# Coupling's twisted partners by transfers that swap partition halves, and two PSUM banks per instruction

## The chip, the cores and the metric

The kernel runs on one core of one Trainium2 chip. The metric is the time of the whole kernel on the device in microseconds (us). Before the change the median of three runs is 1016.11 us (1016.07 to 1016.4).

## What is computed

A chain of two blocks over x of shape (32, 128, 128): causal attention and a gated recurrence with a coupling network (block 0), then experts, a second attention, an adaptive layer and slot attention (block 1). All is float32. The change lies in the coupling of block 0. Its input x is the hidden state of the recurrence:

```python
def _coupling_net(h, w1, b1, w2, b2, w3, b3, w4, b4):
    h = _gelu(h @ w1 + b1)          # 128 -> 128
    h = _gelu(h @ w2 + b2)          # -> 64
    h = _gelu(h @ w3 + b3)          # -> 32
    return jax.nn.sigmoid(h @ w4 + b4)
def _twist(x):
    o_r, o_i, p_r, p_i = jnp.split(x, 4, axis=-1)
    return jnp.concatenate([p_r, -p_i, -o_r, o_i], axis=-1)
gf = _global_net(x.mean(axis=1, keepdims=True), ...)
out = x
for _ in range(3):
    tf = _coupling_net(out, ...)
    coupling = 0.1 + adaptive_range * (0.7 * gf + 0.3 * tf - 0.5) * 2.0
    out = out + coupling * _twist(out)
```

The coupling coefficient is one number per token in tf and one per sequence in gf; the weights are laid out so that all 128 partitions carry it.

## The kernel before, in words

Features lie on the 128 partitions, the 4096 tokens on the free axis, in eight chunks c of 512. Each engine has its own list of instructions, written out by hand; semaphores order them across engines, and also within an engine where one instruction needs another's result. HF is the hidden state (one 512-column piece a chunk), XT holds the twisted state, XF the running sum of the block, PB the eight PSUM banks of 512 columns.

The coupling takes the chunks in four pairs p = 0 to 3 (chunks 2p and 2p+1) and goes through three cycles y = 0 to 2, twelve couplings m = 4y + p. A coupling has five stages, st 0 to 4, and the pairs follow one another one stage apart (`turn_steps`).

- `pe_h1`, `act_g1` (st 0): first layer, one matmul and one Gelu for each chunk of the pair. The matmul of m >= 4 waits for the sum of m - 4 (`s_cs`), the Gelu of m >= 4 for GpSimd's update of m - 4 (`s_ptw`), since it overwrites H1, which that update reads.
- st 1, 2: second and third layer, both chunks in one bank (L941, L946, L973, L976).
- st 3: fourth layer (L951), a bank for each chunk, and Tanh in place (L981), the sigmoid up to scale and shift.
- st 4, VectorE (`dve_couple`), each step once for each chunk of the pair: first the coefficient cp = Tanh x ar03 + cB in PSUM (L994); for y < 2 second cp x state into H1 (L998); third cp x twisted state in PSUM (L1007); fourth the sum with the state into HF (L1012), in the last cycle with XF (L1015).
- st 4, GpSimd (`pool_couple`): twisted state minus H1 (L1026), and in cycle 1 the state added to XF (L1030).

The twisted state of cycle 0 is made by `pe_tw` (L930, a product with a signed permutation) and `act_tw` (L961, a copy from PSUM to XT). Later cycles update it: twist(out + cp x twist(out)) = twist(out) - cp x out.

Beside this run: the recurrence's gates for chunk 7 on VectorE (L494 to L547), which end just ahead of coupling; the global net (`pe_context`, `act_context`, `dve_context`, L600), the first steps of the adaptive layer (`dve_adapt`, L1065 to L1072), and ten weight splits for the experts, ScalarE's part L1087 and GpSimd's part L1092, one a turn. Behind it the experts begin (`pe_up`, L1169, L1174, L1183), while the last coupling, m = 11, is still done on VectorE between their steps. Which PSUM bank a matmul writes is planned by `plan3`: two rings of four banks, one for the small layers, one for the fourth layer and part of the twist.

## Time and profile before

| | us |
|---|---|
| median of three runs | 1016.11 |
| span of the profiled execution | 1016.5 |
| TensorE, VectorE, ScalarE, GpSimd busy | 977.0, 876.8, 831.3, 471.2 |
| block 0 attention and gates | 0 to 455 |
| coupling | 455 to 525 |
| experts | 525 to 707 |
| second attention and on | 707 to 1016.5 |

The profile is one execution. A line of a timeline gives the start and the length in us, the engine, the line of the kernel, the operation with what it writes and reads, and how many instructions were merged; in brackets stands idle time ahead of it and what ended it. Merged instructions can overlap, so the distance between starts tells how fast an engine goes. The experts' up and down matmuls overlap coupling's end from 509 us. Idle time of an engine off the path costs nothing.

### The profile page before, as it was taken

What the parts mean: (1) busy time and instruction counts of PE and PEld (TensorE: products, weight loads), DVE (VectorE), ACT (ScalarE), POOL (GpSimd) and SP (SyncE); (2) the same over time, 40 slices, a digit from 0 to 9 for tenths busy, and PEclk for the clock granted to TensorE, in tenths of its full rate; (3) what the DMA queues carried; (4) which work ended last, traced back from release to release, by engine and by line L of the source; (5) the groups of instructions that cost most, each with busy time, mean ns of one, the idle gap of its engine ahead of it and who ended that gap; (6) DMA issues with size and microseconds to landing.
All of it is one profiled execution on the core that took longest, in us unless ns stands there. A gap on an engine that the chain in (4) does not pass through costs nothing.

```text
span 1016.5 us, 25956 instructions
## 1 busy us (share of the span) xinstructions
PE 977.0 (96%) x8939; PEld 789.2 (78%) x8939; DVE 876.8 (86%) x3718; ACT 831.3 (82%) x2232; POOL 471.2 (46%) x541
## 2 busy tenths in 40 slices
PE   7999999999999999999989999999999999999897
PEld 6898888888888989743268988888777777776566
DVE  6777989898989888799998899889988888896985
ACT  6888888888888888887797878776887888886786
POOL 2334545454545463606810112102887888893041
PEclk9999999999999999999999999999999999999999
DMA  9000000000000000000000000000000000000002
GB/s 376 35 2 2 2 2 2 2 2 2 2 2 2 2 2 2 2 1 0 1 1 1 1 1 1 1 11 11 23 23 23 23 23 23 23 3 1 1 2 84
DMA packets 8723, 18.31 MB, mean 18 GB/s; under 512 B 1296, under 2 KB 5648, under 8 KB 8208
## 3 DMA queue, kind: packets, MB, share of 16 engines
q1 hardware_dynamic: 8592, 16.65, 4.9%
q8 instruction: 71, 1.16, 0.5%
q14 instruction: 60, 0.49, 0.2%
HBM read 10.36 MB, written 2.10 MB: 12 GB/s over the span
## 4 chain that ended last, share of the span: by engine, by line
PE 79%; DVE 9%; ACT 6%; POOL 3%; issue 3%; DMA 0%; DVEq 0%; ACTq 0%; POOLq 0%
PE PB L245 8%; PE PB L246 8%; PE PB L247 8%; PE PB L341 6%; PE PB L396 6%; PE PB L379 6%; PE PB L1798 5%; PE PB L1195 3%; PE PB L1770 3%; PE PB L1197 3%; PE PB L1196 3%; PE PB L1815 3%; PE PB L428 2%; PE PB L429 1%; PE PB L430 1%
## 5 line engine op out<-in xcount | busy, mean ns | idle before, releaser
L371 POOL TENSOR_TENSOR W<-W,small 128x512 f32<-128x512 f32 x128 | 138.5, 1082 | 216.3 <-DVE small L365 216.3
L360 ACT ACTIVATE W<-W,small 128x128 f32<-128x128 f32 x512 | 198.8, 390 | 29.6 <-DVE small L351 29.0
L245 PE MATMUL PB<-RR_s 128*128 128x256 f32 (+3 forms) x568 | 184.4, 325 | 3.5 <-issue 1.9
L246 PE MATMUL PB<-RR_s 128*128 128x256 f32 (+3 forms) x568 | 176.8, 311 | 0.0
L247 PE MATMUL PB<-RR_s 128*128 128x256 f32 (+3 forms) x568 | 176.7, 311 | 0.0
L351 DVE CUSTOM_DVE_ANT_0 W<-PB,W 128x128 f32<-128x128 f32 x512 | 117.3, 284 | 39.1 <-PE PB L341 38.1
L1786 POOL TENSOR_TENSOR AR_s<-AR_s,small 128x512 f32<-128x512 f32 x128 | 129.3, 1040 | 15.9 <-DVE small L1779 15.8
L1169 ACT ACTIVATE AR_s<-PB,W 128x512 f32<-128x512 f32 (+2 forms) x160 | 100.5, 629 | 28.5 <-PE PB L247 22.1
L245 PEld LDWEIGHTS PB<-RR_s 128*128 128x128 f32 x568 | 108.6, 191 | 11.1 <-issue 4.2
L1183 DVE TENSOR_TENSOR RR_s<-AR_s,RR_s 128x512 fp32r<-128x512 f32 (+2 forms) x160 | 100.4, 636 | 17.1 <-ACT RR_s L1174 13.8
L1779 DVE CUSTOM_DVE_ANT_0 AR_s<-PB,W 128x128 f32<-128x128 f32 x512 | 111.0, 286 | 2.6 <-PE PB L1770 0.9
L246 PEld LDWEIGHTS PB<-RR_s 128*128 128x128 f32 x568 | 108.8, 191 | 4.4 <-issue 0.5
L247 PEld LDWEIGHTS PB<-RR_s 128*128 128x128 f32 x568 | 108.4, 191 | 4.9
L360 ACT ACTIVATION_READ_ACCUMULATOR W<-W,small 128x1 f32 x512 | 96.5, 188 | 0.0
L1804 ACT ACTIVATE AR_s<-PB 128x512 f32<-128x512 f32 x128 | 72.6, 592 | 19.4 <-PE PB L1798 19.0
L1791 ACT ACTIVATE AR_s<-AR_s 128x512 f32<-128x512 f32 x128 | 79.7, 625 | 9.6 <-POOL AR_s L1786 9.2
L310 DVE COPY AR_s<-PB 128x512 f32<-128x512 f32 x128 | 86.0, 672 | 1.2 <-PE PB L247 1.2
L379 PE MATMUL PB<-W 128*128 128x128 f32 x512 | 81.4, 281 | 2.6 <-ACT XT L385 2.4
L1798 PEld LDWEIGHTS PB<-W,AR_s 128*128 128x128 f32 x512 | 57.3, 142 | 26.3 <-issue 12.4
L1798 PE MATMUL PB<-W,AR_s 128*128 128x128 f32 x512 | 71.5, 280 | 5.0 <-ACT AR_s L1822 2.5
L385 ACT ACTIVATE XT<-PB 128x512 f32<-128x512 f32 x128 | 74.1, 579 | 1.2 <-PE PB L379 1.2
L341 PE MATMUL PB<-AR_s 64*128 64x128 f32 x1024 | 74.4, 285 | 0.0
(385 smaller groups left out, 2437.0 us busy)
## 6 DMA issues: line engine op xcount, KB each, us to landing
W<-in_w SPq DMA_DIRECT2D x1, 5809.5 KB, 25.5
W<-in_w SPq DMA_DIRECT2D x2, 1024.0 KB, 7.2
out<-XT SPq DMA_DIRECT2D x8, 256.0 KB, 2.3
XF<-in_xT SPq DMA_DIRECT2D x3, 512.0 KB, 10.9
W<-AR_s SPq DMA_DIRECT2D x16, 64.0 KB, 2.1
AR_s<-AR_s SPq DMA_DIRECT2D x16, 64.0 KB, 2.1
QS<-AR_s SPq DMA_DIRECT2D x12, 64.0 KB, 2.1
KR<-AR_s SPq DMA_DIRECT2D x12, 64.0 KB, 2.1
```

The source lines that it names most:

```text
L245: nc.tensor.matmul(out, lh, rh, start=True, stop=False)
L246: nc.tensor.matmul(out, ll, rh, start=False, stop=False)
L247: return nc.tensor.matmul(out, lh, rl, start=False, stop=True)
L341: mm = nc.tensor.matmul(score(u, h), qk[r, b * 128:b * 128 + 128], qk[r, 256 + b * 128:256 + b * 128 + 128], start=True, stop=True)
L351: nc.vector.tensor_tensor_reduce(SS[r][:, hl], score(u, h), w("mask"), 1.0, 3.0e38, ALU.add, ALU.min, mx[r][:, h:h + 1]).then_inc(s_max, 1)
L360: e = nc.scalar.activation(SS[r][:, hl], SS[r][:, hl], ACTF.Exp, bias=mx[r][:, h:h + 1], scale=-1.0, accum_out=rc[r][:, h:h + 1])
L371: nc.gpsimd.tensor_tensor(s3, s3, over(rc[r], 2, [128, 4, 128]), ALU.mult).then_inc(s_nrm, 1)
L379: mm = nc.tensor.transpose(PB[4][:, hl], SS[u % 6][:, hl], ident)
L1169: nc.scalar.activation(G4[k][:, 0:L], PB[k][:, 0:L], ACTF.Gelu_apprx_tanh, bias=b1).then_inc(s_ge, 1)
L1779: nc.vector.tensor_tensor_reduce(SS5[r][:, hl], score5(u, h), w("mask"), isq8, -3.0e38, ALU.subtract, ALU.max, mx5[r][:, h:h + 1]).then_in ...
L1786: nc.gpsimd.tensor_tensor(s3, s3, over(mx5[r], 2, [128, 4, 128]), ALU.subtract).then_inc(s_sub, 1)
L1798: mm = nc.tensor.transpose(bank5(("p", u))[:, hl], SS5[u % 6][:, hl], ident)
```

## The change

The twist matmuls and copies are gone. The partner of cycle 0 comes by transfers, two for each chunk, that write the upper 64 partitions of HF into the lower 64 of XT and the other way round; SyncE issues them once attention is done with XT, and those of pairs 2 and 3 wait for those of pair 0 and 1. The signs of the twist go to the coefficient: a column `tsign` (1, -1, -1, 1 for the four groups of 32 partitions) multiplies ar07, ar03 and the constant 0.1. The update of later cycles stays as it is, because swapping the halves turns the sign of the coefficient. The PSUM banks are now one tensor, and Tanh as well as each of VectorE's steps takes the pair's two banks in one instruction of 1024 columns, with one count of the semaphore for a pair. GpSimd's instructions stay at 512 columns but wait for the pair. The column `twist` of 128 weights becomes `tsign` of 1. The rest of the diff is the counts of the waits, `pe_tw`, `act_tw`, `plan_tw` and their calls taken out, and the plan of banks without them.

```diff
-        PB = [ctx.enter_context(nc.psum_tensor(f"PB{i}", [128, 512], F32)) for i in range(8)]
+        PS = ctx.enter_context(nc.psum_tensor("PB", [128, 4096], F32))
+        PB = [PS[:, i * 512:(i + 1) * 512] for i in range(8)]
...
-            nc.vector.tensor_scalar(cB[:, a:b], gfT[:, a:b], ar07, 0.1, ALU.mult, ALU.add).then_inc(s_cxd, 1)
+            nc.vector.tensor_scalar(cB[:, a:b], gfT[:, a:b], ar07, c01, ALU.mult, ALU.add).then_inc(s_cxd, 1)
...
-                    nc.vector.tensor_scalar(ar07, w("ar"), 0.7, None, ALU.mult).then_inc(s_set, 1)
+                    nc.vector.tensor_scalar(ar07, w("ar"), w("tsign"), 0.7, ALU.mult, ALU.mult).then_inc(s_set, 1)
+                    nc.vector.tensor_scalar(c01, w("tsign"), 0.1, None, ALU.mult).then_inc(s_set, 1)
...
+        def banks3(key):
+
+            n = through3[key + (0,)][1] % 4
+            assert through3[key + (0,)][0] == 1 and through3[key + (1,)][1] % 4 == n + 1
+            return PS[:, (4 + n) * 512:(6 + n) * 512]
...
             if m < 4:
                 pe.wait_ge(s_gd, c * NGD + GFIN)
             else:
-                pe.wait_ge(s_cs, 2 * (m - 4) + s + 1)
+                pe.wait_ge(s_cs, m - 4 + 1)
...
-        def pe_tw(p):
-            for s in range(2):
-                pe.wait_ge(s_gd, (2 * p + s) * NGD + GFIN)
-                pe_drained3(("tw", p, s))
-                nc.tensor.matmul(bank3(("tw", p, s))[:, :], w("twist"), cs(HF, 2 * p + s), start=True, stop=True).then_inc(s_tw, 1)
...
-        def act_tw(p):
-            for s in range(2):
-                act.wait_ge(s_tw, 2 * p + s + 1)
-                nc.scalar.activation(cs(XT, 2 * p + s), bank3(("tw", p, s))[:, :], ACTF.Copy).then_inc(s_twc, 1)
...
-                for s in range(2):
-                    act.wait_ge(s_h4, 2 * m + 2)
-                    nc.scalar.activation(bank3(("h4", m, s))[:, :], bank3(("h4", m, s))[:, :], ACTF.Tanh, bias=b4h2, scale=0.5).then_inc(s_tn, 1)
+                act.wait_ge(s_h4, 2 * m + 2)
+                nc.scalar.activation(banks3(("h4", m)), banks3(("h4", m)), ACTF.Tanh, bias=b4h2, scale=0.5).then_inc(s_tn, 1)
...
+            cp = banks3(("h4", m))
+            if 0 in steps:
+                dve.wait_ge(s_tn, m + 1)
+                nc.vector.scalar_tensor_tensor(v8(cp), v8(cp), ar03, over(cB[:, 8 * p:8 * p + 8], 2, [128, 8, 128]), ALU.mult, ALU.add).then_inc(s_cp, 1)
             if y < 2 and 1 in steps:
-                for s, cp in enumerate(cps):
-                    dve.wait_ge(s_cp, 2 * m + s + 1)
-                    nc.vector.tensor_tensor(cs(H1[p], s), cp, cs(S, s), ALU.mult).then_inc(s_ct, 1)
...
+                dve.wait_ge(s_cp, m + 1)
+                nc.vector.tensor_tensor(H1[p], cp, S, ALU.mult).then_inc(s_ct, 1)
+            if 2 in steps:
+                dve.wait_ge(s_cp, m + 1)
                 if y == 0:
-                    dve.wait_ge(s_twc, 2 * p + s + 1)
+                    dve.wait_ge(s_tw[p % 2], 64 * (p // 2) + 64)
                 else:
-                    dve.wait_ge(s_ptw, 2 * m + s - 8 + 1)
+                    dve.wait_ge(s_ptw, 2 * (m - 4) + 2)
                 if y < 2:
-                    dve.wait_ge(s_ct, 2 * m + s + 1)
-                nc.vector.tensor_tensor(cp, cp, cs(Tw, s), ALU.mult).then_inc(s_cu, 1)
...
+                    dve.wait_ge(s_ct, m + 1)
+                nc.vector.tensor_tensor(cp, cp, Tw, ALU.mult).then_inc(s_cu, 1)
+            if 3 in steps:
+                dve.wait_ge(s_cu, m + 1)
                 if y < 2:
-                    nc.vector.tensor_tensor(cs(S, s), cp, cs(S, s), ALU.add).then_inc(s_cs, 1)
+                    nc.vector.tensor_tensor(S, cp, S, ALU.add).then_inc(s_cs, 1)
...
             for s in range(2):
-                i = 2 * m + s
-                pool.wait_ge(s_ct, i + 1)
-                pool.wait_ge(s_cu, i + 1)
+                pool.wait_ge(s_ct, m + 1)
+                pool.wait_ge(s_cu, m + 1)
                 nc.gpsimd.tensor_tensor(cs(Tw, s), cs(Tw, s), cs(H1[p], s), ALU.subtract).then_inc(s_ptw, 1)
...
         def sp_layers():
+            sp.wait_ge(s_pv, NV)
+            for p in range(4):
+                if p >= 2:
+                    sp.wait_ge(s_tw[p % 2], 64)
+                for c in (2 * p, 2 * p + 1):
+                    sp.wait_ge(s_gd, c * NGD + GFIN)
+                    nc.sync.dma_start(cs(XT, c)[0:64, :], cs(HF, c)[64:128, :]).then_inc(s_tw[p % 2], 16)
+                    nc.sync.dma_start(cs(XT, c)[64:128, :], cs(HF, c)[0:64, :]).then_inc(s_tw[p % 2], 16)
```

## Rows read from the trace of the kernel before

**Rows 1.** The page's first line.
```profile
span 1016.5 us, 25956 instructions
```

**Rows 2.** Busy time of each engine in a stretch, then granted clock, DMA share, GB/s.
```profile
455.00:481.00 26.00, 24.85 (x74) 8.32 (x75) 25.90 (x46) 20.49 (x38) 16.81 (x16) 1.00 0.00 0
...
525.00:707.00 182.00, 181.83 (x913) 159.14 (x914) 163.12 (x317) 144.73 (x251) 22.32 (x22) 1.00 0.01 4
```

**Rows 3.** Timeline of VectorE, coupling m = 0 and the steps behind it.
```profile
455.36 1.40 DVE L994 SCALAR_TENSOR_TENSOR PB<-PB,small 128x512 f32<-128x512 f32 x2
456.67 1.28 DVE L998 TENSOR_TENSOR AR_s<-PB,HF 128x512 f32<-128x512 f32 x2
457.86 1.28 DVE L1007 TENSOR_TENSOR PB<-PB,XT 128x512 f32<-128x512 f32 x2
459.06 1.28 DVE L1012 TENSOR_TENSOR HF<-PB,HF 128x512 f32<-128x512 f32 x2
460.25 1.01 DVE L1065 TENSOR_SCALAR small<-W,small 32x128 f32<-32x128 f32 x1
461.29 0.28 DVE L1067 TENSOR_TENSOR small<-small,W 32x128 f32<-32x128 f32 x1
...
461.82 1.40 DVE L994 SCALAR_TENSOR_TENSOR PB<-PB,small 128x512 f32<-128x512 f32 x2
...
466.82 0.85 DVE L600 TENSOR_SCALAR small<-small 128x8 f32<-128x8 f32 x1
```

**Rows 4.** Timeline of GpSimd: the updates of m = 0, 4 and 7.
```profile
458.69 2.49 POOL L1026 TENSOR_TENSOR XT<-XT,AR_s 128x512 f32<-128x512 f32 x2 [1.15 <-DVE PB L1007]
...
481.31 2.49 POOL L1026 TENSOR_TENSOR XT<-XT,AR_s 128x512 f32<-128x512 f32 x2
...
499.17 2.51 POOL L1026 TENSOR_TENSOR XT<-XT,AR_s 128x512 f32<-128x512 f32 x2
```

**Rows 5.** Timeline of ScalarE: first layer of m = 11, Tanh of m = 11.
```profile
501.76 1.26 ACT L956 ACTIVATE AR_s<-PB,W 128x512 f32<-128x512 f32 x2 [1.89 <-POOL XT L1026]
...
509.06 1.24 ACT L981 ACTIVATE PB<-PB,small 128x512 f32<-128x512 f32 x2 [0.22 <-PE PB L951]
```

**Rows 6.** Groups by line and shape, 430 to 525: busy us, mean ns, idle before.
```profile
L1012 DVE TENSOR_TENSOR HF<-PB,HF 128x512 f32<-128x512 f32 x16 | 10.2, 673 | 0.0
...
L930 PE MATMUL PB<-HF,W 128*128 128x512 f32 x16 | 7.7, 612 | 0.0
...
L961 ACT ACTIVATE XT<-PB 128x512 f32<-128x512 f32 x8 | 4.5, 586 | 1.3 <-PE PB L930 1.3
...
L439 DVE TENSOR_TENSOR XF<-PB,XF 128x256 f32<-128x256 f32 x2 | 0.8, 412 | 0.2 <-PE PB L430 0.2
...
L454 ACT ACTIVATE RR_s<-XF 128x256 fp32r<-128x256 f32 x1 | 0.4, 416 | 0.8 <-DVE XF L439 0.8
```

**Rows 7.** The page, DMA issues: KB each, median us to landing.
```profile
out<-XT SPq DMA_DIRECT2D x8, 256.0 KB, 2.3
```

**Rows 8.** Timeline of VectorE: two steps, each waiting for the one before.
```profile
440.71 0.69 DVE L502 TENSOR_TENSOR AR_s<-AR_s 128x512 f32<-128x512 f32 x1
441.44 0.69 DVE L504 TENSOR_TENSOR AR_s<-AR_s 128x512 f32<-128x512 f32 x1
```

**Rows 9.** Timelines of GpSimd and VectorE in attention, 269 to 273 us.
```profile
269.62 1.04 POOL L371 TENSOR_TENSOR W<-W,small 128x512 f32<-128x512 f32 x1 [0.98 <-DVE small L365]
270.62 1.46 POOL L565 TENSOR_TENSOR SM<-HF,W 128x512 f32<-128x512 f32 x1
...
270.04 0.91 DVE L515 TENSOR_SCALAR W<-W 128x512 f32<-128x512 f32 x1
...
270.96 1.40 DVE L459 TENSOR_TENSOR RR_s<-XF,RR_s 128x256 fp32r<-128x256 f32 x1
```

**Rows 10.** Busy time by stretch, near the end: PE first, the clock after POOL.
```profile
951.00:952.00 1.00, 0.29 (x2) 0.05 (x1) 0.97 (x6) 0.56 (x4) 0.00 (x0) 1.00 0.00 0
...
953.00:954.00 1.00, 1.00 (x9) 0.67 (x9) 0.86 (x7) 0.68 (x3) 0.00 (x0) 0.50 0.00 0
```

More of the change, by code:

```diff
@@ L805, in build @@
         s_set3 = signal("cpl_setup")
-        s_h1, s_tw, s_h2, s_h3, s_h4 = signal("h1"), signal("twist"), signal("h2"), signal("h3"), signal("h4")
-        s_g1, s_twc, s_g2, s_g3, s_tn = signal("g1"), signal("twisted"), signal("g2"), signal("g3"), signal("tn")
+        s_h1, s_h2, s_h3, s_h4 = signal("h1"), signal("h2"), signal("h3"), signal("h4")
+        s_g1, s_g2, s_g3, s_tn = signal("g1"), signal("g2"), signal("g3"), signal("tn")
+        s_tw = [signal(f"twisted{p}") for p in range(2)]
         s_cp, s_cu, s_ct, s_cs, s_x2 = signal("cpl"), signal("cpl_u"), signal("cpl_t"), signal("cpl_s"), signal("x2")
@@ L890, in used @@
         def used(m, s):
[L892 removed]
+            return (s_cs, m + 1) if m < 8 else (s_x2, m - 8 + 1)
         def plan_small(t):
@@ L965, in act_couple @@
             if y:
-                act.wait_ge(s_cs, 2 * (m - 4) + 2)
+                act.wait_ge(s_cs, m - 4 + 1)
                 act.wait_ge(s_ptw, 2 * (m - 4) + 2)
@@ L978, in act_couple @@
                 act.wait_ge(s_set3, 1)
-                for s in range(2):
-                    act.wait_ge(s_h4, 2 * m + 2)
-                    nc.scalar.activation(bank3(("h4", m, s))[:, :], bank3(("h4", m, s))[:, :], ACTF.Tanh, bias=b4h2, scale=0.5).then_inc(s_tn, 1)
+                act.wait_ge(s_h4, 2 * m + 2)
+                nc.scalar.activation(banks3(("h4", m)), banks3(("h4", m)), ACTF.Tanh, bias=b4h2, scale=0.5).then_inc(s_tn, 1)
         def dve_couple(p, y, st, steps=range(4)):
@@ L989, in dve_couple @@
             dve.wait_ge(s_cxd, 1 if p < 3 else 4)
-            cps = [bank3(("h4", m, s))[:, :] for s in range(2)]
-            for s, cp in enumerate(cps if 0 in steps else ()):
-                c = 2 * p + s
-                dve.wait_ge(s_tn, 2 * m + s + 1)
-                nc.vector.scalar_tensor_tensor(v4(cp), v4(cp), ar03, over(cB[:, 4 * c:4 * c + 4], 2, [128, 4, 128]), ALU.mult, ALU.add).then_inc(s_cp, 1)
-            if y < 2 and 1 in steps:
-                for s, cp in enumerate(cps):
-                    dve.wait_ge(s_cp, 2 * m + s + 1)
-                    nc.vector.tensor_tensor(cs(H1[p], s), cp, cs(S, s), ALU.mult).then_inc(s_ct, 1)
@@ L999, in dve_couple @@
-            for s, cp in enumerate(cps if 2 in steps else ()):
-                dve.wait_ge(s_cp, 2 * m + s + 1)
+            cp = banks3(("h4", m))
+            if 0 in steps:
+                dve.wait_ge(s_tn, m + 1)
+                nc.vector.scalar_tensor_tensor(v8(cp), v8(cp), ar03, over(cB[:, 8 * p:8 * p + 8], 2, [128, 8, 128]), ALU.mult, ALU.add).then_inc(s_cp, 1)
+            if y < 2 and 1 in steps:
+                dve.wait_ge(s_cp, m + 1)
+                nc.vector.tensor_tensor(H1[p], cp, S, ALU.mult).then_inc(s_ct, 1)
@@ L1008, in dve_couple @@
-            for s, cp in enumerate(cps if 3 in steps else ()):
-                c = 2 * p + s
-                dve.wait_ge(s_cu, 2 * m + s + 1)
+                    dve.wait_ge(s_ct, m + 1)
+                nc.vector.tensor_tensor(cp, cp, Tw, ALU.mult).then_inc(s_cu, 1)
+            if 3 in steps:
+                dve.wait_ge(s_cu, m + 1)
                 if y < 2:
-                    nc.vector.tensor_tensor(cs(S, s), cp, cs(S, s), ALU.add).then_inc(s_cs, 1)
+                    nc.vector.tensor_tensor(S, cp, S, ALU.add).then_inc(s_cs, 1)
@@ L1013, in dve_couple @@
                 else:
-                    dve.wait_ge(s_pxs, c + 1)
-                    nc.vector.tensor_tensor(cs(XF, c), cp, cs(XF, c), ALU.add).then_inc(s_x2, 1)
+                    dve.wait_ge(s_pxs, 2 * p + 2)
+                    nc.vector.tensor_tensor(cs(XF, p, 1024), cp, cs(XF, p, 1024), ALU.add).then_inc(s_x2, 1)
         def pool_couple(p, y, st):
@@ L1164, in act_up @@
             if n == 0:
-                act.wait_ge(s_x2, 2 * (k // 2) + 2)
+                act.wait_ge(s_x2, k // 2 + 1)
             else:
@@ L1576, in pool_layers @@
             pool.wait_ge(s_dn, 4 * 19)
-            pool.wait_ge(s_cu, 24)
+            pool.wait_ge(s_cu, 12)
             nc.gpsimd.memset(HX, 0.0).then_inc(s_hx, 1)
@@ L2810, in pack @@
     row("ar", inp["L0_ffn_adaptive_range"])
-    tw = np.zeros((128, 128), f)
-    r = np.arange(32)
-    tw[64 + r, r] = 1
-    tw[96 + r, 32 + r] = -1
-    tw[r, 64 + r] = -1
-    tw[32 + r, 96 + r] = 1
-    put("twist", tw)
+    col("tsign", np.repeat(np.array([1, -1, -1, 1], f), 32))
     put("gatew", blocks(inp["L1_cond_gate_w"], 3))
```

27 lines of the change are left out of this document (6 added, 21 removed), and 2 rows, old and new, of the table COLS.

## The prediction

> Numbering: pair p (0 to 3) holds chunks 2p and 2p+1, cycle y is 0 to 2, and m = 4y + p counts the twelve couplings. "Third instruction" is the product with the twisted half (L1007), "fourth" the sum (L1012 or L1015).
>
> **What bounds the kernel now.** The profiled execution spans 1016.5 us [rows 1]; the three timed runs have a median of 1016.11, so I work on the span and take 0.4 off at the end. I read the busy time by stage first [rows 2]: the reader is to see that the stretch in which coupling runs, 455 to 525 us, is the only part this change touches, and that behind it, from 525 to 707, TensorE is busy 181.83 of 182 us. So the change is worth what it moves the start of that stage, and nothing that is saved on an engine counts otherwise. From 455 to 481 VectorE is busy 25.90 of 26 us, TensorE 24.85.
>
> Next the timelines, engine by engine. VectorE's [rows 3]: coupling m = 0 starts at 455.36 and the next step behind it at 460.25, with no idle time; the two halves of each of its four steps overlap, so that the starts lie 1.31, 1.19, 1.20 and 1.19 us apart, 4.89 in all. GpSimd's [rows 4]: its update of the twisted half comes 0.15 us after the first half of the third instruction (457.86 + 0.68, then 458.69). From 481.31 (m = 4) to 499.17 (m = 7) it never stops: three turns in 17.86 us, 5.95 each, longer than VectorE's 4.89. Here GpSimd is the bound. ScalarE's [rows 5]: the last first-layer Gelu pair starts at 501.76, 1.89 us of idle time ended by GpSimd (499.17 + 2.51 = 501.68), and the last Tanh pair, at 509.06 for 1.24 us, leads into the experts. So the path is: VectorE for m = 0 to 3, GpSimd for m = 4 to 7, ScalarE and VectorE by turns to 525, then TensorE.
>
> **Removed: the twist on TensorE and ScalarE.** Sixteen matmul passes, 7.7 us busy, and eight copies, 4.5 us busy [rows 6]. They lie at 440 to 461 us. VectorE is busy there by its own chain (the gates of chunk 7) and starts m = 0 when that chain ends, not when Tanh is done, so this is worth 0 by itself. If the cover were gone, the first coupling could start earlier; it isn't.
>
> **Added: sixteen transfers on SyncE's queue.** Nearest row: 256 KB land in 2.3 us [rows 7]; these are 128 KB each. The queue waits for the last attention product (about 433 us), then for chunk 7's gates (about 454). The first are needed at 457.86, those of chunk 7 at m = 3, some 15 us later. In four groups of four, at 2.3 us a group and a little for their issue, they take 9 to 12 us and end before 446, apart from chunk 7's, about 457. Behind them on the queue are only the spreading transfers of the next attention, which come at the end of the experts' stage. Cost 0, at the worst 0 too unless one took over 15 us.
>
> **VectorE's pairs in one instruction.** An instruction of 128x256 takes 412 ns, of 128x512 673 [rows 6], so 512 more columns cost 0.52 us. Two bounds. If nothing waited, a pair would save one start: 1.19 - 2 x 0.52 = 0.15 us at the most, by the overlap seen more like 0.06; over 44 pairs 2.8 us at 0.06. But the steps depend on each other. Today's second half hides the end of the first: cp(0) is finished while cp(1) runs. Fused, each step waits for the one directly before it. The trace shows such a chain: 128x512 instructions that each need the one before start 0.73 us apart (440.71, 441.44), each 0.69 long [rows 8]; a wait on one's predecessor thus costs the full duration plus 0.04, against 0.60 when the halves overlap. So a fused turn is (0.74 + 0.53 + 0.04) + 2 x (0.68 + 0.53 + 0.04) + (0.68 + 0.53 - 0.07) = 1.31 + 2.50 + 1.14 = 4.95 us: 0.06 more than 4.89. I take this, as rows 8 is the same kind of instruction with the same kind of wait; the range runs from -0.37 a turn (no wait paid) to +0.1.
>
> The Trainium skill (VectorE: DVE Perf Modes, section on the TRN2 errata) says that the SBUF latency is paid between instructions and that one large tile pays it once, which speaks for the fusion. By that rule, without the dependency, the estimate is the lower bound above; the trace agrees on the fixed cost, and rows 8 says who pays it.
>
> **Whoever waits for a half now waits for both.** GpSimd starts behind the whole third instruction: 1.31 + 1.25 + 1.21 + 0.15 = 3.92 us into the turn, against 458.69 - 455.36 = 3.33 now: +0.59. The first-layer matmuls of the next cycle and the next coupling's start behind Tanh wait in the same way; for m up to 6 they have 0.7 us or more of slack.
>
> **The shared port.** After m = 0 VectorE does three small steps of another part (L1065, L1067, L1069), after m = 1 a copy and L600. L1065, a 32x128 instruction, takes 1.01 us and ends at 461.26, and L600, 128x8, 0.85, ending at 467.67 [rows 3]: both end just as GpSimd's second update does (458.69 + 2.49 = 461.18). In attention the same is seen from both sides [rows 9]: L515 takes 0.91 and ends 0.3 us behind GpSimd's instruction of 269.62, in between it and the next, which takes 1.46; and L459, with two SBUF operands, takes 1.40 for 256 columns and ends behind that one. So VectorE slips in between two of GpSimd's. Now GpSimd's two updates come 0.59 later and the small steps fall on them differently. After m = 0: L1065 gets in at GpSimd's first boundary, but L1067 reads two SBUF tensors and waits for the end of the second update, some 461.85, and m = 1 starts at about 462.3, now 461.82 [rows 3]: +0.5. After m = 1: L600 comes 5.04 us into the turn (3.80 + 1.14 + 0.10), GpSimd's first boundary is at 3.92 + 1.22 = 5.14; it gets in there instead of waiting for the second: 0.6 less than now for that wait. m = 2 starts at about 467.7, +0.1, m = 3 +0.15.
>
> The Trainium skill (SBUF — State Buffer, Who interferes with whom) states the same lock: two-port modes and instructions with two SBUF inputs contend with GpSimd, and whoever issues first has the pair for the whole instruction.
>
> **ScalarE's Tanh pairs.** A copy of 256 columns takes 416 ns, of 512 586 [rows 6], 0.35 us for 512 more at most 0.41. A pair in 1.24 becomes 1.01 to 1.07, and starts what follows 0.2 sooner. Only the last three (m = 9, 10, 11) lie on the path: -0.6. The first of the two halves is no longer out early: VectorE waits 0.37 longer at m = 8 and 9.
>
> **The sum.** GpSimd begins m = 3 at +0.15 + 0.59 = +0.7. That goes through the Gelu of m = 7 and a weight split to GpSimd's m = 4, 482.0 for 481.31, and its run to 501.68 keeps it: the last Gelu pair starts at 502.46. ScalarE gives back 0.6 and enters the experts at +0.1. VectorE is at +1.07 at m = 9, makes up 0.3 in a wait for ScalarE that goes (a split of chunk 0), and at m = 10 and 11, where expert steps stand between its fused ones and no step waits for its predecessor, about 0.6. That leaves +0.15 at 520 us, and TensorE's stage keeps it. Other edits (one 128x1 instruction more at 44 us, pointer scalars for constants, 127 columns less to load): 0. Span 1016.65, median 1016.3.
>
> **Rivals.**
> *The port is missed (slower).* L600's margin is 0.10 us (5.04 against 5.14), less than my terms are good for. If it comes later it waits for the second update, 1.22 more. For it: a margin this thin. Against: it holds at the durations in the rows. The other place is L1069: without the twist, ScalarE reaches its weight split sooner, GpSimd can follow its second update with that split at once, and L1069, again two SBUF operands, waits for it, 1.1 us. It decides if the split is ready by 461.9; I get 461.5 if TensorE's clock is full. Either one: +1.0, 1017.3. Both: +2.1 to 2.3, 1018.4.
> *Fusing pays (faster).* If a wait on the direct predecessor costs less for instructions that stay in PSUM, a turn takes 4.95 - 0.37 = 4.58; m = 3 starts 1.0 sooner, GpSimd's term shrinks by 0.3, and the sum is -1.2: 1014.9. Against it: rows 8. A full 2.8 us (1013.3) would need GpSimd off the path from 481 on, where the rows show it without a gap.
> *TensorE's clock.* It is at full in all of coupling. Later in the trace, after a microsecond with 0.29 us of matmuls (951 to 952), it was 0.50 at 953 to 954, the 1.2 GHz level [rows 10]. Without the twist TensorE lacks 7.7 us of work from 440 to 461 and by my count stands still for about 4 us before 454.9. A low stretch that ends by 466 costs nothing (Tanh of m = 2 has 5 us in hand), and it would even keep the split of the first rival late. One in the turns after that, where TensorE works 24.85 of 26 us, loses half its length; two stretches like the trace's, 3.2 us long, give +3: 1019.3.
> *The transfers don't do their work in time*: no chance to speak of, above.
>
> **Chances.** Forecast 0.50; one port hit 0.20; both 0.13; fusing pays 0.12; clock 0.05. A measurement of this kernel can tell some 0.2%, 2.0 us, from no change: below 1014.1 is faster, above 1018.1 slower. Faster: under half of the third rival, 0.05. Slower: most of "both" and the clock, 0.13. Same: 0.82. The range reaches to the faster rival and to both port hits: 1014.6 to 1018.4.
>
> **What would show it.** Right: the fused steps of a turn start about 1.31, 1.25 and 1.25 apart, with a turn of 4.95; GpSimd's update starts 3.9 us into the turn; from m = 4 GpSimd runs without a gap, started near 482.0; the last Gelu pair near 502.5; no slower matmuls in coupling but perhaps around 455. Wrong: starts 1.13 apart (fusing pays); m = 1 later than 462.8 or m = 2 later than 468.3 (port); L924 at twice its 0.48 us a pass after 466 (clock); a Tanh of 1024 columns over 1.1 us, which would take the tail's gain.

## The result, and the profile after

| | before | changed |
|---|---|---|
| median of 21 runs each, taken in turn | 1017.46 | 1018.61 |
| ratio, 95% interval | | 1.0013, 1.0007 to 1.0019 |
| span of the profiled execution | 1016.5 | 1017.3 |
| coupling's length | 56.26 | 58.91 |

The change made the kernel slower by 1.15 us (0.7 to 1.9), which is under what my chances counted as a difference, and the time lies 0.2 us above the range. Two things add to it. The kernel before had a median of 1017.46 here, 1.35 above the 1016.11 of the three runs that the forecast stood on. And the change cost 1.15 where I forecast 0.2. The first is spread between runs of one kernel: the three runs of the forecast are the first three of these 21, and all three lie among its lower ones. The second is the subject of this part. "Length" is from now on the time from the first coupling step on VectorE to the experts' first Gelu on ScalarE (455.36 to 511.62 us before). It repeats within 0.05 us from one profiled execution to the next (before: 56.26, 56.30, 56.30; changed: 58.91, 58.89), so it can settle terms of tenths, which the time itself can't. The forecast put it at +0.15; it is +2.65.

The page's first line for the changed kernel, to set against [rows 1]:
```profile
span 1017.3 us, 25853 instructions
```
VectorE's timeline from m = 0 to the start of m = 2, to set against [rows 3]:
```profile
455.70 1.27 DVE L982 SCALAR_TENSOR_TENSOR PB<-PB,small 128x1024 f32<-128x1024 f32 x1
457.00 1.22 DVE L985 TENSOR_TENSOR AR_s<-PB,HF 128x1024 f32<-128x1024 f32 x1
458.33 1.23 DVE L994 TENSOR_TENSOR PB<-PB,XT 128x1024 f32<-128x1024 f32 x1
459.60 1.22 DVE L998 TENSOR_TENSOR HF<-PB,HF 128x1024 f32<-128x1024 f32 x1
460.74 0.33 DVE L1050 TENSOR_SCALAR small<-W,small 32x128 f32<-32x128 f32 x1
461.10 1.24 DVE L1052 TENSOR_TENSOR small<-small,W 32x128 f32<-32x128 f32 x1
462.37 0.28 DVE L1054 TENSOR_TENSOR small<-small,W 32x128 f32<-32x128 f32 x1
462.58 1.27 DVE L982 SCALAR_TENSOR_TENSOR PB<-PB,small 128x1024 f32<-128x1024 f32 x1
...
467.63 0.18 DVE L1057 COPY small<-PB 128x32 f32<-128x32 f32 x1
467.73 1.39 DVE L601 TENSOR_SCALAR small<-small 128x8 f32<-128x8 f32 x1
469.03 1.28 DVE L982 SCALAR_TENSOR_TENSOR PB<-PB,small 128x1024 f32<-128x1024 f32 x1
```
The four steps start 1.30, 1.33, 1.27 and 1.14 us apart: 5.04, against 4.89 before. The small steps behind m = 0 cost what they were forecast to: m = 1 starts 6.88 after m = 0. The step at 467.73 is the one of the forecast's thin margin, and it took 1.39 instead of about 0.2, so that m = 2 starts 13.33 after m = 0 (12.23 before).

GpSimd's timeline, the updates of m = 0, 4 and 7 and a weight split, to set against [rows 4]:
```profile
459.71 2.49 POOL L1011 TENSOR_TENSOR XT<-XT,AR_s 128x512 f32<-128x512 f32 x2 [1.65 <-DVE PB L994]
...
482.58 1.27 POOL L1077 TENSOR_TENSOR RR_s<-W,RR_s 128x512 fp32r<-128x512 f32 x1 [0.75 <-ACT RR_s L1072]
483.81 2.50 POOL L1011 TENSOR_TENSOR XT<-XT,AR_s 128x512 f32<-128x512 f32 x2
...
502.21 2.50 POOL L1011 TENSOR_TENSOR XT<-XT,AR_s 128x512 f32<-128x512 f32 x2
```
The first update comes 4.01 into the turn (3.33 before). From 483.81 to 502.21 there is no gap, but three turns take 18.40 us, 6.13 each for 5.95: the weight split in each takes 1.27 us where it took 1.09 before. No term of my sum had that.

ScalarE's timeline, the last first-layer pair, the last Tanh and the experts' first Gelu, to set against [rows 5]:
```profile
504.79 1.26 ACT L951 ACTIVATE AR_s<-PB,W 128x512 f32<-128x512 f32 x2 [2.22 <-POOL XT L1011]
...
512.20 1.09 ACT L970 ACTIVATE PB<-PB,small 128x1024 f32<-128x1024 f32 x1 [0.61 <-PE PB L946]
...
514.61 0.69 ACT L1154 ACTIVATE AR_s<-PB,W 128x512 f32<-128x512 f32 x1
```
From 504.79 to 514.61 it is 9.82 us, and 9.86 before (501.76 to 511.62). The tail of ScalarE, in which three shorter Tanh pairs were to give back 0.6, gave back 0.04.

Busy time by stretch around coupling's start, PE first, the granted clock behind POOL:
```profile
452.00:454.00 2.00, 0.00 (x0) 0.00 (x0) 1.97 (x8) 0.17 (x1) 0.00 (x0) 0.59 0.00 0
456.00:458.00 2.00, 2.00 (x4) 0.68 (x2) 1.97 (x2) 0.67 (x1) 1.92 (x3) 0.50 0.27 57
460.00:462.00 2.00, 1.98 (x8) 0.36 (x5) 1.97 (x3) 0.69 (x1) 2.00 (x2) 1.00 0.00 0
```
TensorE stood still before 455 and was then granted the 1.2 GHz level until 459, as the forecast allowed for. What it cost is the subject of two runs below.

### The profile page after: what moved, and what is told of

Read it like the earlier page. It is cut to its first block, busy times and chain, and to the rows that moved or that the text cites. A ratio compares the mean times of both kernels' runs of the same rounds, so it can differ in the third digit from the quotient of the medians.

```text
span 1017.3 us, 25853 instructions
## 1 busy us (share of the span) xinstructions
PE 970.7 (95%) x8923; PEld 786.5 (77%) x8923; DVE 878.2 (86%) x3675; ACT 825.0 (81%) x2212; POOL 472.6 (46%) x541
## 4 chain that ended last, share of the span: by engine, by line
PE 78%; DVE 10%; ACT 6%; POOL 3%; issue 2%; DMA 0%; DVEq 0%; ACTq 0%; POOLq 0%
PE PB L246 8%; PE PB L247 8%; PE PB L248 8%; PE PB L342 6%; PE PB L397 6%; PE PB L380 6%; PE PB L1783 5%; PE PB L1180 3%; PE PB L1181 3%; PE PB L1182 3%; PE PB L1755 3%; PE PB L1800 3%; PE PB L429 2%; PE PB L430 1%; PE PB L431 1%
```

## Experiments: taking the 2.65 us apart

Times of the table come from the unrounded trace and can differ by 0.01 from differences of the lines shown. In it, m1, m2 and G4 are the starts of m = 1, of m = 2 and of GpSimd's update of m = 4, G the last first-layer pair on ScalarE, all after the first coupling step. Ratios are to the kernel before, run in turn with each, over 10 or 11 runs (21 for the changed kernel). A kernel without a ratio ran once, under the profiler: e_immediate took 1018.63, e_tail 1018.20, e_third 1017.91 and e_twistmm 1020.84 us.

| kernel | m1 | m2 | G4 | G | length | ratio |
|---|---|---|---|---|---|---|
| before | 6.46 | 12.23 | 25.96 | 46.40 | 56.26 | |
| changed | 6.89 | 13.34 | 28.11 | 49.10 | 58.91 | 1.0013 |
| e_pad | 6.89 | 13.34 | 27.93 | 48.40 | 58.21 | 1.0015 (1.0005 to 1.0024) |
| e_immediate | 6.89 | 12.16 | 26.76 | 47.22 | 57.03 | |
| e_fused | 6.89 | 12.16 | 26.76 | 47.21 | 57.02 | 1.0005 (0.9993 to 1.0017) |
| e_transfers | 6.46 | 12.24 | 25.97 | 46.42 | 56.28 | 0.9995 (0.9984 to 1.0006) |
| e_twistmm | 6.89 | 13.34 | 27.94 | 48.38 | 58.20 | |
| e_tail | 6.89 | 12.17 | 26.77 | 47.21 | 56.89 | |
| e_small | 5.72 | 12.64 | 27.24 | 47.68 | 57.50 | 1.0004 (0.9994 to 1.0013) |
| e_third | 5.78 | 12.77 | 27.85 | 48.29 | 58.17 | |
| e_best | 5.77 | 10.67 | 27.63 | 48.07 | 57.76 | 1.0012 (1.0003 to 1.0021) |
| e_copyback | 5.78 | 10.78 | 25.50 | 45.94 | 55.62 | 0.9987 (0.9978 to 0.9996) |
| changed again | 6.89 | 13.33 | 28.11 | 49.08 | 58.89 | 1.0018 (1.0009 to 1.0027) |

**The columns (e_pad).** The theory was formed on the profile after: the only thing that the change did to a weight split is to move the weights and tiles by 127 columns.
```diff
-    ("gw1", 64), ("gw2", 32), ("gw3", 128), ("gb1", 1), ("gb2", 1), ("gb3", 1), ("ar", 1), ("tsign", 1),
+    ("gw1", 64), ("gw2", 32), ("gw3", 128), ("gb1", 1), ("gb2", 1), ("gb3", 1), ("ar", 1), ("tsign", 1), ("spare", 127),
```


> The changed kernel with 127 unused columns behind tsign, so that every later weight lies at the column it had before. GpSimd's weight splits took 1.09 us each before and 1.27 in the changed kernel, ten of them, and only where their operands lie differs. Theory 'columns': here they take 1.09 again; four of them lie in GpSimd's gapless run behind the third coupling, so coupling's length falls by 4 x 0.18 = 0.7 us, from 58.9 to 58.2, and the time by 0.7 us. Rival 'lock': the splits are longer because they now meet other VectorE instructions at the shared port; then they stay at 1.27 and the length at 58.9.

Measured: splits of 1.09 us and a length of 58.21, 0.70 less. The group of the ten splits, in the changed kernel and then in e_pad (busy us, then mean ns of one):
```profile
L1077 POOL TENSOR_TENSOR RR_s<-W,RR_s 128x512 fp32r<-128x512 f32 x10 | 12.7, 1272 | 2.3 <-ACT RR_s L1072 2.3
```
```profile
L1077 POOL TENSOR_TENSOR RR_s<-W,RR_s 128x512 fp32r<-128x512 f32 x10 | 10.9, 1088 | 2.5 <-ACT RR_s L1072 2.5
```
The same instruction on the same sizes takes GpSimd 0.18 us longer when its operands start 127 columns earlier. The time can't tell: 1.0015 here and 1.0013 for the changed kernel, each with an interval of 0.6 to 1 us on either side.

**Transfers alone (e_transfers).** The kernel before, in halves, with the transfers and signs in place of the twist, and 128 columns.
```diff
-                nc.tensor.matmul(bank3(("tw", p, s))[:, :], w("twist"), cs(HF, 2 * p + s), start=True, stop=True).then_inc(s_tw, 1)
...
-                nc.scalar.activation(cs(XT, 2 * p + s), bank3(("tw", p, s))[:, :], ACTF.Copy).then_inc(s_twc, 1)
...
+                    nc.sync.dma_start(cs(XT, c)[0:64, :], cs(HF, c)[64:128, :]).then_inc(s_tw[p % 2], 16)
+                    nc.sync.dma_start(cs(XT, c)[64:128, :], cs(HF, c)[0:64, :]).then_inc(s_tw[p % 2], 16)
```


> The kernel before with the transfers and the signs in the coefficients, but VectorE and ScalarE in halves as before (columns padded as before). Theory 'fusing costs': everything lost comes from the pairs in one instruction and the columns, so this one is at the level of before or a little below: coupling's length 56.0 to 56.4 us, time within 0.3 us of before, with the clock low around 452 to 460 as in the changed kernel, but absorbed. Rival 'idle TensorE costs': the missing 7.7 us of matmuls and the half clock from 452 to 459 delay coupling; then the length is 57 us or more and the time 1 us or more above before.

Length 56.28: the whole removal of TensorE's and ScalarE's twist is worth 0.02, as forecast, and the half clock at 452 (it was there too, for 6.8 us) costs nothing.

**Fusing alone (e_fused).** The other half of the change: pairs in one instruction on VectorE and ScalarE, the twist left on TensorE, the columns of before.
```diff
-            for s, cp in enumerate(cps if 2 in steps else ()):
...
-                nc.vector.tensor_tensor(cp, cp, cs(Tw, s), ALU.mult).then_inc(s_cu, 1)
...
+            if 2 in steps:
...
+                nc.vector.tensor_tensor(cp, cp, Tw, ALU.mult).then_inc(s_cu, 1)
```


> The kernel before with VectorE's steps and Tanh taking a pair's two banks at once, but the twist by matmul and copy as before (same columns as before). Theory 'fusing costs': turns of 5.05 us on VectorE, GpSimd's update 4.0 us into the turn, the small steps after the first and second coupling hit GpSimd as in the changed kernel; the length is 58.2 us (58.9 less 0.7 for the columns), time +1.9 us. Rival 'the twist's removal costs': VectorE's turns lengthen by 0.1 but the length stays under 57 us.

The turns and GpSimd's start came as expected, the length did not: 57.02, not the 58.2 of e_pad (and +0.5 us of time, not +1.9). Transfers cost nothing, and yet 1.19 us were missing. The place is one instruction. VectorE's timeline behind m = 1 of this kernel:
```profile
465.92 0.18 DVE L1075 COPY small<-PB 128x32 f32<-128x32 f32 x1
466.01 0.22 DVE L601 TENSOR_SCALAR small<-small 128x8 f32<-128x8 f32 x1
466.14 1.28 DVE L1000 SCALAR_TENSOR_TENSOR PB<-PB,small 128x1024 f32<-128x1024 f32 x1
```
Here the 128x8 step took 0.22 us. This step's code differs from the changed kernel's only in that 0.1 is an immediate; there it is the tile c01, because the transfers' signs multiply it.

**One pointer scalar (e_immediate).** e_pad with that alone. A pointer scalar is a constant that the instruction reads from a tile of 128x1, one value a partition; an immediate stands in the instruction itself.
```diff
-            nc.vector.tensor_scalar(cB[:, a:b], gfT[:, a:b], ar07, c01, ALU.mult, ALU.add).then_inc(s_cxd, 1)
+            nc.vector.tensor_scalar(cB[:, a:b], gfT[:, a:b], ar07, 0.1, ALU.mult, ALU.add).then_inc(s_cxd, 1)
```


> The changed kernel with the 127 unused columns, and in the 128x8 step behind m = 1 (and its 128x24 twin) the constant 0.1 as an immediate instead of the 128x1 tile c01, so that the instruction reads one pointer scalar (ar07) as in the kernel before. The sign on the constant is left out, so half of the coupling's constants have the wrong sign; no time hangs on that. Theory 'two pointer scalars make it miss the port' (worked out from the run with fused steps and the twist kept, where this step took 0.22 us and m = 2 started 12.16 after m = 0, and from the run with 127 columns, where it took 1.39 and m = 2 started at 13.34): the step takes about 0.2, m = 2 starts at 12.2, and coupling's length (first coupling step to the experts' first Gelu) falls from 58.21 to 57.0. Rival 'the transfers or the missing twist moved something else by 0.1 us' : the step still ends with GpSimd's second update (1.4 us), m = 2 at 13.3, length 58.2.

m = 2 at 12.16 and length 57.03, on the spot. Two timelines show how little is between them: first e_pad's VectorE, then its GpSimd with the second update of m = 1 by itself.
```profile
466.86 1.39 DVE L601 TENSOR_SCALAR small<-small 128x8 f32<-128x8 f32 x1
```
```profile
466.95 1.27 POOL L1011 TENSOR_TENSOR XT<-XT,AR_s 128x512 f32<-128x512 f32 x1
```
And e_immediate's VectorE, then both of GpSimd's updates (the second by itself starts at 467.26 in the trace):
```profile
467.17 0.22 DVE L601 TENSOR_SCALAR small<-small 128x8 f32<-128x8 f32 x1
```
```profile
466.04 2.49 POOL L1011 TENSOR_TENSOR XT<-XT,AR_s 128x512 f32<-128x512 f32 x2 [1.72 <-DVE PB L994]
```
Both steps start 0.09 us ahead of GpSimd's second instruction. With one pointer scalar VectorE is through at 467.39; with two it ends at 468.25, just behind GpSimd's instruction (466.95 + 1.27 = 468.22). That the step waits for GpSimd's instruction to end is what the trace shows; that the second pointer scalar makes it ask for the port a few hundredths too late is my reading, and no run varies the start by hundredths or puts another tile in the place of c01. What speaks for it is the step's twin of 128x24 elements, which runs just ahead of coupling while GpSimd stands idle: 0.23 us with one pointer scalar (before, e_fused, e_immediate), 0.29 with two (changed, e_pad, e_transfers).

**TensorE's clock (e_twistmm).** e_pad with sixteen passes of the same size back on TensorE, their result unread, so that it doesn't stand still.
```diff
+                nc.tensor.matmul(bank3(("tw", p, s))[:, :], w("cw1"), cs(HF, 2 * p + s), start=True, stop=True).then_inc(s_h2, 1)
```


> The changed kernel with the 127 unused columns, and the sixteen passes of the twist back on TensorE at their old places, each over the same columns, but with another matrix as weights and with a result that nobody reads (ScalarE's copies stay away). Theory 'TensorE's idle time before 455 us is what brought the half clock there': the 3.4 to 6.8 us at 1.2 GHz that begin at 452 to 455 us in the changed kernel and in both runs with transfers are gone, as in the run with the twist kept, and since they had cost nothing, turns and length stay (58.2). Rival 'the low stretch costs something that the other differences hide': the length falls by 0.3 or more without it.

No half clock near 452 (the same two microseconds as above):
```profile
452.00:454.00 2.00, 2.00 (x9) 0.43 (x10) 1.97 (x7) 1.69 (x2) 0.00 (x0) 1.00 0.00 0
```
The length is 58.20. One execution alone would be thin, but the fifteen profiled ones agree: all ten without the twist's passes have a half-clock stretch that begins between 451 and 455 us (in e_small at 442), and none of the five with passes there has one. So TensorE's idle time is what brings the low clock there. It costs coupling nothing: the stretch lasted 6.8 us in the changed kernel and 3.4 in its second profile, with lengths of 58.91 and 58.89. This kernel's single time of 1020.84 is not explained by coupling: against e_pad's profile it is 1.2 us longer ahead of coupling and 1.6 behind it, where it has a half-clock stretch at 763 us (see the same kernels again, below).

**The tail (e_tail).** e_immediate with VectorE's last cycle in halves, and Tanh in halves for m = 8 and 9. What led to it is TensorE's timeline of e_immediate: the last h4 matmuls wait for VectorE's fused sum of m = 9, whose banks they take.
```profile
508.59 1.13 PE L946 MATMUL PB<-HR,W 32*128 32x512 f32 x4 [1.23 <-DVE XF L1001]
```
```diff
+                if m in (8, 9):
+                    for s in range(2):
+                        nc.scalar.activation(bank3(("h4", m, s))[:, :], bank3(("h4", m, s))[:, :], ACTF.Tanh, bias=b4h2, scale=0.5).then_inc(s_tn, 1)
...
+            if y == 2:
...
+                for s in range(2) if 3 in steps else ():
...
+                    nc.vector.tensor_tensor(cs(XF, c), cs(cp, s), cs(XF, c), ALU.add).then_inc(s_x2, 1)
```


> The kernel with one pointer scalar (length 57.03, the half of the constants' signs left out as there), and in the last cycle (m = 8 to 11) VectorE in halves again, Tanh in halves for m = 8 and 9, in pairs for 10 and 11. The stretch from the last first-layer Gelu pair to the experts' first Gelu was 9.81 there and 9.86 with halves, although three Tanh pairs are 0.15 shorter each. Theory 'the last Tanh waits for VectorE's fused sum of m = 9, whose banks it needs': with that sum in halves and earlier the last Tanh hangs on ScalarE's own Gelu again, the stretch falls to about 9.55 and the length to 56.8. Rival 'the gain of a Tanh pair is taken by something on ScalarE itself': stretch stays at 9.8 and length at 57.0.

TensorE's row of e_tail for the same matmuls waits for ScalarE's Gelu, as it did before the change:
```profile
508.56 1.13 PE L946 MATMUL PB<-HR,W 32*128 32x512 f32 x4 [0.87 <-ACT HR L966]
```
The stretch from G to the experts fell from 9.81 to 9.68 and the length to 56.89, half of what I expected. The mechanism shows in the row. Its size comes out of ScalarE's timelines. In e_immediate each of the three Tanh pairs lets the next instruction start 0.15 us sooner than two halves do, 0.45 in all, and the last Tanh comes 0.40 later by the wait for the banks. In e_tail that wait is gone, but Tanh of m = 9 is in halves again and its 0.15 is lost, which I had not counted; 0.30 is left of the gain, and 0.18 of it was measured against before (9.68 for 9.86). Where the other 0.12 goes I have not followed.

## Experiments: what holds the start of GpSimd's run

**Small steps inside the couplings (e_small).** e_pad with the steps behind m = 0 and m = 1 moved between their second and third instruction.
```diff
+                                dve_couple(p, y, st, (0, 1))
+                                dve_adapt(t)
+                                if t == 6:
+                                    dve_context(24, 32, 4)
+                                dve_couple(p, y, st, (2, 3))
```


> The changed kernel with the 127 unused columns; the three small steps behind m = 0 and the two behind m = 1 now stand inside these couplings, between the second and the third instruction, where GpSimd does nothing or a weight split's last tenths. Nothing else moves. Theory 'the port waits are what the small steps cost': the 32x128 product falls from 1.24 to about 0.3 us and the 128x8 step from 1.39 to about 0.25; m = 1 starts about 5.9 after m = 0 (now 6.89) and m = 2 at about 11.2 (now 13.34). GpSimd's m = 4 then comes some 2 us sooner (now 27.93) if VectorE alone brings it there, and the length is 56.1 to 56.4. Rival 'GpSimd's start at m = 4 hangs on ScalarE's weight split too' : the turns shorten as said but the length falls by 1 us or less, to 57.2 or more.

Inside m = 0 it went as said (m1 5.72, the 32x128 product 0.28 us). Inside m = 1 the copy and the 128x8 step came before their own inputs. VectorE's timeline:
```profile
463.55 0.19 DVE L1057 COPY small<-PB 128x32 f32<-128x32 f32 x1 [0.85 <-PE PB L1031]
464.48 0.29 DVE L601 TENSOR_SCALAR small<-small 128x8 f32<-128x8 f32 x1 [0.74 <-ACT small L594]
```
1.59 us of waiting in place of 1.19 at the port: neither of the two theories, a miss of mine, since the earlier profile had both producers in it.

**The third instruction in halves (e_third).** e_small with the product in two halves and a signal for each.
```diff
-                nc.vector.tensor_tensor(cp, cp, Tw, ALU.mult).then_inc(s_cu, 1)
+                if y < 2:
+                    for s in range(2):
+                        nc.vector.tensor_tensor(cs(cp, s), cs(cp, s), cs(Tw, s), ALU.mult).then_inc(s_cu, 1)
```


> As the run before it (small steps inside m = 0 and m = 1), and in the first eight couplings the third instruction in two halves of 512 columns again, each with its own signal, so that GpSimd's update may start behind the first half. Theory 'whoever waits for a half now waits for both costs 0.6': GpSimd's first update starts 3.5 us into the later turns instead of 4.0, VectorE's turn stays at 5.05 (the second half hides the first half's end, the fourth instruction still waits for its predecessor), and the length falls by 0.5 to 0.6 below that of the run before. Rival 'GpSimd at m = 4 waits for something else by then' : updates start 3.5 into the turns of m = 0 to 3, but m = 4 to 7 stay where they were and the length changes by under 0.2.

The update of m = 2 starts 3.49 into its turn, as said, but the length rose by 0.67. GpSimd's m = 4 waits for a weight split, that for ScalarE's Gelu of m = 7, and that now for its first-layer matmul, which needs the fourth instruction of m = 3. GpSimd's row in e_third, then the same in e_small:
```profile
481.76 1.09 POOL L1081 TENSOR_TENSOR RR_s<-W,RR_s 128x512 fp32r<-128x512 f32 x1 [1.53 <-ACT RR_s L1076]
```
```profile
480.63 1.09 POOL L1077 TENSOR_TENSOR RR_s<-W,RR_s 128x512 fp32r<-128x512 f32 x1 [0.93 <-ACT RR_s L1072]
```
So the two hand-overs of a turn lie side by side: undoing the one leaves the other, the turn grew by 0.07, and 0.35 more went at m = 3, where VectorE stands idle for 0.46 us ahead of the third instruction; all that it waits for had ended by then as far as the trace shows, so the reason is open. That undoing only the first hand-over can't help is read from these rows; no run undoes both on fused steps.

**A version with all of it (e_best).** Transfers, columns, VectorE in halves; the small steps of m = 0 inside m = 0, those of m = 1 inside m = 2; Tanh in pairs for m = 10 and 11.
```diff
+                            if st == 4 and t in (5, 7):
+                                dve_couple(p, y, st, (0, 1))
+                                dve_adapt(5 if t == 5 else 6)
```


> Transfers instead of the twist, the 127 unused columns, VectorE in halves as in the kernel before; the three small steps of behind m = 0 stand inside m = 0 and the two of behind m = 1 inside m = 2, each time between the second and the third instruction; ScalarE takes a pair in one Tanh for m = 10 and 11 alone. Theory (every length here is made of port waits, hand-overs and ScalarE's tail): m = 1 starts 5.5 after m = 0 (before 6.46), m = 2 at 10.4 (12.23), m = 3 at 15.7 (17.13), GpSimd's m = 4 at 24.5 (25.96), the last first-layer Gelu pair at 45.0 (46.40), the length is 54.6 (before 56.26); the time falls by 1.5 us, a ratio near 0.9985. Rival 'GpSimd at m = 4 is held by ScalarE or TensorE instead': turns as said, but the length stays above 55.6.

m2 was 10.67, but m = 3 came 1.55 us late and the length was 57.76, far from the 54.6 expected and 1.50 above the kernel before. The 128x32 copy also frees a PSUM bank; moved by a turn, it holds a first-layer matmul, and with it ScalarE. TensorE's row, then VectorE's m = 3:
```profile
468.76 1.96 PE L924 MATMUL PB<-HF,W 128*128 128x512 f32 x4 [2.09 <-DVE small L1064]
```
```profile
472.75 1.42 DVE L986 SCALAR_TENSOR_TENSOR PB<-PB,small 128x512 f32<-128x512 f32 x2 [1.55 <-ACT PB L973]
```

**The copy put back (e_copyback).** The same, with only the 128x8 step inside m = 2.
```diff
-                                dve_adapt(5 if t == 5 else 6)
+                                if t == 5:
+                                    dve_adapt(t)
```


> The kernel before's halves with the transfers and the small steps moved, but the 128x32 copy that frees a PSUM bank stands behind m = 1 again, as in the kernel before; the 128x8 step stays inside m = 2 and the three 32-row steps inside m = 0. In the run without this, the copy stood inside m = 2, a first-layer matmul waited 2.09 us for its bank, Tanh of m = 3 came 1.55 us too late, and the length was 57.76. Theory 'that bank was the cause': the matmul starts 1 us or more sooner than with the twist's transfers alone (11.69 after m = 0), m = 3 starts at 16.2 to 16.6 (before 17.13) and the length falls to 55.2 to 55.7, with a time 0.6 to 1.1 us below the kernel before's. Rival 'ScalarE itself holds m = 3': m = 3 at 17.1 or later and a length of 56.2 or more.

The matmul and m = 3 start without idle time. TensorE's row, then VectorE's:
```profile
466.21 1.98 PE L924 MATMUL PB<-HF,W 128*128 128x512 f32 x4
```
```profile
470.75 1.39 DVE L986 SCALAR_TENSOR_TENSOR PB<-PB,small 128x512 f32<-128x512 f32 x2
```
m = 3 at 15.88, length 55.62, and a time of 0.9987 (0.9978 to 0.9996) of the kernel before: 1015.81 against 1017.48. The bank was the cause. Two figures came out otherwise than expected: m = 3 came sooner than 16.2, and the matmul only 0.35 us sooner than in e_transfers (11.34 for 11.69), not 1. It is the only version whose time lies clearly below the kernel before. What that rests on can be read against e_transfers, which has the same halves and transfers: G went from 46.42 to 45.94 by the small steps out of GpSimd's way, and the stretch behind G from 9.86 to 9.68 with Tanh in pairs for m = 10 and 11. So 0.48 of the 0.66 us is the small steps, and 0.18 is fusion, on ScalarE alone.

## Experiments: the same kernels again

> The kernel before, unchanged, profiled once more. The question is TensorE's clock. In the first profile of before it was at half from 761 to 765 us (second attention), where the changed kernel's profile has none, and the changed kernel lost its lead of 1.6 us there: its lag was 2.93 us up to 761 and 1.35 behind. Theory 'chance': such stretches fall differently in each execution, so this profile has its low stretches elsewhere or fewer, and its span is up to 1.6 us off 1016.5 on either side, while coupling's length (start of the first coupling to start of the experts' first Gelu) is again 56.3 us. Rival 'fixed': the low stretch at 761 belongs to this kernel and comes again at the same place; then the change really saves 1.6 us there.

> The kernel before, unchanged, for another look at how the granted clock falls: two profiled executions had a half-clock stretch of 3.4 us that starts at 760 to 761 us, none of the changed kernel or of most of its relatives has. 'Fixed by the program': it comes again. 'Chance': it is missing, and the time behind it is 1.5 us shorter than in those.

> The changed kernel, unchanged, beside the others of this call. Length 58.9 again, first low stretch at 452 again. 'Fixed by the program': no half-clock stretch at 761; 'chance': it may have one. Ratio to the kernel before 1.001 to 1.002 either way.

The kernel before had its half-clock stretch at 761 us in two of three profiled executions, the changed kernel in neither of two. Busy time just ahead of it and in it, in the profile of before, then the latter two microseconds in e_before2, which has none:
```profile
758.00:760.00 2.00, 0.42 (x4) 0.18 (x2) 2.00 (x20) 2.00 (x6) 2.00 (x3) 1.00 0.00 0
761.00:763.00 2.00, 2.00 (x36) 1.83 (x34) 1.14 (x4) 1.78 (x4) 2.00 (x4) 0.60 0.00 0
```
```profile
761.00:763.00 2.00, 1.77 (x32) 1.61 (x36) 0.77 (x5) 2.00 (x5) 2.00 (x3) 1.00 0.00 0
```
TensorE is busy in the stretch, but just ahead of it had worked only 0.42 of 2 us. Such a pause does not always bring one; e_fused has it too, and keeps the full clock:
```profile
758.00:760.00 2.00, 0.23 (x2) 0.23 (x3) 1.74 (x15) 2.00 (x5) 2.00 (x3) 1.00 0.00 0
760.00:762.00 2.00, 2.00 (x41) 1.71 (x40) 0.99 (x4) 2.00 (x5) 2.00 (x3) 1.00 0.00 0
```
Over all fifteen profiled executions it appeared in five, at 760 to 763 us: twice in before, in e_immediate, e_tail and e_twistmm, with the twist on TensorE and without it. Span less the start of coupling and its length is 504.7 to 505.3 us in these five and 502.7 to 503.7 in the other ten. Five of the ten, e_before2 and e_after2 among them, have a stretch of 3.4 us at half clock at 510 to 512 us instead, where coupling ends: it changed neither the length (56.30 and 58.89, as without it) nor what comes behind (502.9 to 503.6). "Fixed by the program" is out, and a stretch at 761 is worth about 1.7 us. That is why the profile's span rose by 0.8 only: +0.3 before coupling, +2.65 in it, -2.2 behind it, most of which is this stretch, present in the one and absent in the other. What decides it is open. It reaches the timed runs as well: of the 74 runs of the kernel before in the four later comparisons, 13 had a mean granted clock of 0.998, which is some 4 us at half clock in the whole run, and all 13 took 1014.8 to 1016.3 us, while the medians of the others were 1017.2 to 1017.9.

Does length carry to the time? The eight comparisons have lengths of -0.64, +0.02, +0.76, +1.24, +1.50, +1.95 and +2.65 (the last twice) against before, and times of -1.3, -0.5, +0.5, +0.4, +1.2, +1.5, +1.3 and +1.8 us (ratio less 1, by 1017). Each is uncertain by 0.6 to 1.2 us. They rise together; a straight line through the eight has a slope of 0.86, and the data would bear 1 as well as 0.7.

## Why the prediction was right or wrong

Right, with their runs:
- *Removed twist 0, transfers 0*: 0.02 together (e_transfers).
- *The clock*: low around 455, gone by 460, worth 0 (e_twistmm, e_transfers).
- *Port behind m = 0*: m = 1 forecast 6.9 into coupling, measured 6.89; the 32x128 product waits for GpSimd's second update. The rival's other place, the last of the three steps, did not come (0.28 us). By the Trainium skill (SBUF — State Buffer, Who interferes with whom) an instruction with two SBUF inputs contends with GpSimd and the loser blocks for the whole instruction; the trace agrees (1.24 us there, 0.28 in e_small, where GpSimd stood still).
- *Hand-over to GpSimd* and its way through the Gelu of m = 7: +0.7 forecast for its m = 4, +0.80 measured in e_immediate, where port and columns are out of the way (26.76 against 25.96), of it 0.68 by waiting for the pair (forecast 0.59) and 0.09 by the turns. This split is read from the timelines; the one run that tried to undo the wait for the pair, e_third, ran into another.

Nearly right: *the fused turn*, 4.95 forecast, 5.05 measured. The second and fourth steps pay the 0.04 of [rows 8]; the third pays 0.11 (458.33 against 457.00 + 1.22). It waits for more than its predecessor, which may be why; no run varies it. The sign held: with four dependent steps fusing costs 0.15 a turn where two overlapping halves hid it, so the rival "fusing pays" falls (4.58 would have been its turn). Two slips in that part of the forecast change nothing: 44 pairs at 0.06 make 2.6, not 2.8, and the -0.37 a turn is taken once from 4.89 and once from 4.95.

Wrong, in order of size:
- *Port behind m = 1* (0 forecast, +1.19 measured). The place and the price (1.22) stand in the first rival, with a chance of 0.20. But its reason was lateness, and the step wasn't late: 0.09 us were left (467.73, GpSimd at 467.82), as forecast. The step that failed is the last line of the sum, "other edits (..., pointer scalars for constants, ...): 0". It was put at nothing without a reason; it should have been priced by what stood within 0.1 us behind it. Shown by e_immediate, which differs from e_pad in that scalar alone: m2 12.16 for 13.34, length 57.03 for 58.21.
- *127 columns less* (0 forecast, +0.70 measured). The same line. I had called it less to load; it moved operands of the engine that bounds m = 4 to 7, and each weight split took 1.27 us for 1.09 (e_pad).
- *The tail* (-0.6 forecast, -0.04 measured). A Tanh pair took 1.09 us, and what follows started 0.15 sooner for each of the three instead of 0.2, so the term was worth 0.45 at most. The other 0.40 went because TensorE's last h4 needs the banks of m = 9, whose fused sum ends at once for both, and later: VectorE stood at +1.24 there in e_immediate. The chain had changed engines. That wait is seen in e_immediate and gone in e_tail; e_tail got back 0.13 of the length.

The sum: 0.15 forecast + 1.19 + 0.70 + 0.56 and 0.05 of small ones make 2.65. On the time, the miss was 2.31 us, and 1.35 of it were the level of the kernel before; three runs within 0.3 us of each other had looked like a firm base, but single runs of that kernel lay between 1014.8 and 1019.7 in the comparisons here. The range had no room for that: its upper end was both port hits on the low base. It was luck, on the other hand, that the time rose by only 1.15 us where the length rose by 2.65. In the profiles most of the difference is the stretch at 761 us, which the forecast did not have; how much of it the timed runs owe to that is open.

## What to carry to other kernels

Fusing two halves into one instruction saves a start and loses the overlap: where each step needs the one before it, and other engines wait for halves, it costs (here 0.15 us a turn and 0.68 at a hand-over). When small VectorE steps stand beside GpSimd's long ones, put them where GpSimd is idle and their inputs are ready, and see what else they release, a PSUM bank for one: here that took 0.48 us off the path, where the whole change had added 2.65. Edits "without a price", a pointer for a constant or a layout that shifts by a few columns, are to be priced at the place with the thinnest margin.

## What the runs showed of the hardware

- A GpSimd TENSOR_TENSOR of 128x512 took 1.09 us or 1.27 us by the columns at which its operands start, 127 apart; the updates of XT took 1.27 in all kernels.
- A VectorE instruction of 128x8 that starts 0.09 us ahead of GpSimd's next one gets in between (0.22 us) or waits for it (1.39) by whether it has one or two pointer scalars (e_immediate, e_pad). With GpSimd idle the same form on 128x24 takes 0.23 and 0.29.
- The half-clock stretch at 761 us comes and goes between executions of one program (2 of 3) and is worth about 1.7 us of 1016. TensorE worked 0.42 of the 2 us ahead of it, and 0.23 of them in e_fused, where none followed. One of 3.4 us at 510 us cost nothing that can be measured.
- TensorE at 1.2 GHz for 6.8 us from 452 on cost coupling nothing: the length was 58.91, and 58.89 with a stretch of 3.4 us.
